# The attention's state product in a mixture-of-experts layer: one product of 128 columns written as four of 32

## What is computed

```python
def step(S, inp):
    q_t, k_t, v_t, gk_t = inp
    S = jnp.exp(gk_t)[..., None] * S + k_t[..., None] * v_t[..., None, :]
    o_t = jnp.einsum('bhdv,bhd->bhv', S, q_t) * SCALE
    return (S, o_t)
...
o = o * jax.lax.rsqrt(jnp.mean(o * o, axis=-1, keepdims=True) + EPS) * g_norm_w
o = o.reshape(Bb, Ll, Hid)
g = x @ Wg
o = o * (g * jax.nn.sigmoid(g))
o = o @ Wo
...
h = h + _L0_attn_ref(_layernorm(h, axis=-1), ...)
h = h + _L0_ffn_ref(_layernorm(h, axis=-1), ...)
```

## Time and profile before

| | |
|---|---|
| median of three runs | 635.37 us |
| lowest, highest | 631.81, 639.4 us |
| span of the profiled execution | 629.6 us |
| its own device time | not listed apart from the runs; the median stands 5.8 us above the span |
| PE matmuls busy | 585.3 us, 93% |
| PE weight loads busy | 548.2 us, 87% |
| DVE, ACT, GpSimd busy | 379.6, 337.5, 308.1 us |
| mean granted TensorE clock | 0.974 |

### The profile page before, as it was taken

One profiled execution on the slowest core, in us unless ns is written; L12 is line 12 of the kernel. 1 busy time (PEld: TensorE's weight loads), 2 busy tenths in 40 slices (PEclk: granted clock), 3 DMA queues, 4 the chain that ended last, 5 costly groups with the idle time before them and its releaser, 6 DMA issues.

```text
span 629.6 us, 14269 instructions
## 1 busy us (share of the span) xinstructions
PE 585.3 (93%) x5044; PEld 548.2 (87%) x5044; DVE 379.6 (60%) x1000; ACT 337.5 (54%) x889; POOL 308.1 (49%) x370
## 2 busy tenths in 40 slices
PE   5999999999989989739999999999999999999993
PEld 5998889789977776538899999999999999999993
DVE  4756668877765869745553736637457275473540
ACT  4687678546666756223464626537356274462530
POOL 6002222110545188534176967568575775767323
PEclk9999999999999999865999999999999999999998
DMA  7992012012313001121565171550824607333003
GB/s 206 276 320 90 12 41 89 4 60 68 118 39 104 23 22 35 52 79 56 181 197 106 47 222 18 176 108 22 236 26 144 140 1 246 38 89 54 10 7 42
DMA packets 44875, 59.89 MB, mean 95 GB/s; under 512 B 5184, under 2 KB 33424, under 8 KB 44816
## 3 DMA queue, kind: packets, MB, share of 16 engines
q1 hardware_dynamic: 37136, 49.28, 25.5%
q0 software_dynamic: 7680, 9.86, 9.2%
HBM read 41.07 MB, written 18.05 MB: 94 GB/s over the span
## 4 chain that ended last, share of the span: by engine, by line
PE 87%; DVE 5%; issue 3%; ACT 1%; another core or an unknown queue 1%; DMA 0%; DVEq 0%; POOL 0%; SPq 0%; POOLq 0%
PE ps L1928 49%; PE ps L1975 14%; PE ps L2150 3%; PE ps L2164 3%; PE ps L2109 3%; PE ps L1970 2%; PE ps L2054 2%; PE ps L2145 2%; PE ps L1949 1%; PE ps L2179 1%; PE ps L2157 1%; PE ps L2125 1%; PE ps L2072 1%; DVE sb_att L1698 1%; PE ps L2198 1%
## 5 line engine op out<-in xcount | busy, mean ns | idle before, releaser
L1928 PE MATMUL ps<-sb_xe_hi,sb_rounded 128*128 128x256 f32 (+1 forms) x1024 | 211.2, 299 | 0.2 <-DVE sb_dec L1433 0.2
L1928 PEld LDWEIGHTS ps<-sb_xe_hi,sb_rounded 128*128 128x128 f32 x1024 | 167.4, 190 | 3.0 <-issue 2.3
L1928 PE MATMUL ps<-sb_xe_lo,sb_rounded 128*128 128x320 f32 (+1 forms) x512 | 151.7, 296 | 0.0
L1928 PEld LDWEIGHTS ps<-sb_xe_lo,sb_rounded 128*128 128x128 f32 x512 | 97.2, 190 | 0.0
L1433 DVE TENSOR_TENSOR sb_dec<-ps,sb_gate 128x256 f32<-128x256 f32 (+1 forms) x121 | 55.2, 456 | 66.8 <-ACT sb_gate L1135 61.2
L1975 PE MATMUL ps<-sb_rounded,sb_h_hi 128*128 128x256 f32 x512 | 94.3, 285 | 0.0
L1135 ACT ACTIVATE sb_gate<-ps 128x256 f32<-128x256 f32 (+1 forms) x121 | 49.2, 406 | 71.8 <-PE ps L1928 70.9
L1975 PEld LDWEIGHTS ps<-sb_rounded,sb_h_hi 128*128 128x128 f32 x512 | 78.2, 189 | 0.0
L980 POOL DMA_INDIRECT out_rows<-sb_att,sb_s_token x40 | 61.8, 1545 | 28.1 <-DVE sb_att L1444 19.2
L1975 PE MATMUL ps<-sb_rounded,sb_h_lo 128*128 128x256 f32 x256 | 71.9, 281 | 0.0
L1463 DVE TENSOR_TENSOR sb_h_lo<-sb_dec,sb_h_hi 128x256 fp32r<-128x256 f32 x128 | 66.5, 520 | 1.9 <-ACT sb_h_hi L1398 1.1
(11 more groups left out here) (216 smaller groups left out, 1110.9 us busy)
## 6 DMA issues: line engine op xcount, KB each, us to landing
sb_x_in<-in_x SPq DMA_DIRECT2D x16, 512.0 KB, 4.8
sb_raw<-in_L_ffn_W SPq DMA_DIRECT2D x16, 512.0 KB
sb_x_in<-in_L_ffn_W SPq DMA_DIRECT2D x16, 512.0 KB
xe_rows<-sb_xr SPq DMA_DIRECT2D x3, 1457.5 KB, 14.2
sb_att<-xe_rows SPq DMA_DIRECT2D x32, 132.5 KB, 2.3
sb_xn<-in_L_ffn_W SPq DMA_DIRECT2D x8, 512.0 KB
sb_h<-in_L_ffn_W SPq DMA_DIRECT2D x8, 512.0 KB
out_rows<-sb_h SPq DMA_DIRECT2D x16, 128.0 KB, 2.1
```

The lines of the kernel that those rows point to most:

```text
L1928: ins = pe.matmul(out_ap, lhs, rhs, start=(first and i == 0), stop=(last and i == n - 1))
```

## The change

It touches the mix on PE alone. For a tile of 128 tokens the state's product of 128 columns becomes four products of 32 columns, each of which writes its strip of 32 partitions, as the attention's products do; each is put ahead of its half's 8 products. For the tile of 32 tokens the product stays as it is, but those of both halves now stand ahead of all the others. Only the first half's state product starts the accumulation in the bank (`start=(hf == 0)`). What is multiplied and added is the same.

```diff
                     else:
                         need("pool", "q_mask", b, 0)
                         need.once(consts, CONSTS)
+                    old = state[:, c % 2, :, :] if c else state0[:, b % 2, :, :]
+                    queries = zq[b % 2][:, :, ST[c]:ST[c] + r]
+                    if r < P:
+                        for hf in range(DT):
+                            pe.matmul(bank[:, hf * r:(hf + 1) * r], old[:, hf, :], queries[:, hf, :],
+                                      start=(hf == 0), stop=False, skip_group_check=True)
                     for hf in range(DT):
                         cols = slice(hf * r, (hf + 1) * r)
-                        pe.matmul(bank[:, cols], state[:, c % 2, hf, :] if c else state0[:, b % 2, hf, :],
-                                  zq[b % 2][:, hf, ST[c]:ST[c] + r], start=True, stop=False, skip_group_check=True)
+                        for j in range(4 if r == P else 0):
+                            at_j = slice(32 * j, 32 * j + 32)
+                            pe.matmul(bank[at_j, cols], old[:, hf, at_j], queries[:, hf, :],
+                                      start=(hf == 0), stop=False, skip_group_check=True)
                         for e in range(2):
                             for j in range(4):
                                 v48 = vp[b % 2][0:r, c, 4 * hf + j, :, :].rearrange("p a v -> p (a v)")
```

## The result

| measured | median us (lowest to highest) | kernel before beside it | ratio, 95% interval |
|---|---|---|---|
| the change | 635.11 (629.28 to 644.4) | 637.89 | 0.9924 [0.9898, 0.9951] |
| again (`after_again`) | 633.97 (630.69 to 640.08) | 637.61 | 0.9965 [0.9936, 0.9993] |
| a third time (`after_third`) | 635.03 (628.45 to 639.39) | 637.7 | 0.9954 [0.9902, 1.0006] |

A forecast was written before the change was run, and what follows sets the result against it. PE was taken to bound the kernel, busy nearly throughout 8 to 228 us. Terms 5.3 + 0.7 + 0.8 + 0.3 + 1.3 = 8.4 us, 3.4 lost, 5.0 off 635.37 gives 630.4 us; range 625.5 to 637.

The forecast's parts named there:

- Inside the full mixes, 0.33 each: In each of 16 full mixes the pair of shape changes between the halves goes: 0.33 us each, 5.3 on PE.
- Behind another mix: Two mixes directly behind another mix also lose the pair of shape changes between them: 2 x 0.33 = 0.7 us.
- Behind scores: Four mixes following a scores step start attention 0.22 us behind the state product instead of 0.42: 4 x 0.20 = 0.8 us.
- The 32-token tiles, 0.34 each: Four tiles of 32 tokens, both wide state products put ahead of all narrow records: 0.34 us saved each, 1.3 in all.
- The hand-overs: Places after 97 us where PE waits for just-in-time suppliers, mostly DVE; 3.4 us of PE's gain lost there.
- 5.0 of 8.4 pass: Of 8.4 us saved on PE over all mixes, 5.0 reach the kernel's end.
- Rival 4, code fetch, 0.12: Added instructions shift PE's code-fetch stops: one more of 2.4 us gives 632.8, one fewer 628; chance 0.12 with more stops.
- Rival 3, the sequencer: In the mixes the sequencer cannot feed the denser records: 10.6 us slower on PE, 642 at the end; chance 0.07.
- the rule weighed there: Skill's about 62 ns per MATMUL: a full mix 3.0 us against 2.0, kernel some 15 us slower; trace judged against it.
- Rival 1, everything passes: All of PE's 8.4 us saving in the mixes reaches the end, giving 627.0 us; chance 0.17.
- PE's busy time down by 8: Sign that the forecast is right: PE's busy time over the profile falls by some 8 us.
- Experts 5 us earlier: Sign that the forecast is right: the experts, after the attention and routing, begin some 5 us earlier.

The follow-up runs named there:

- batch3: The kernel before with the change made in batch 3's mixes alone; ratio to the kernel before 0.998 [0.9933, 1.0027].
- after_shift: The change with 96 TensorE instructions fewer inside batch 0's never-taken exact path; 630.74 us, ratio to the kernel before 0.9869.
- hoist_wide: The kernel before with both 128-column state products of every mix put ahead of its narrow products, not split; 633.48 us, ratio 0.9917.
- before_shift: The kernel before with 160 TensorE instructions fewer inside batch 0's never-taken exact path; 638.92 us, ratio 1.0006.
- hoist_b0: The change, but batch 0's state products stay wide, ahead of its narrow ones; 631.08 us, ratio to the kernel before 0.9871; again 631.33, 0.988.
- before_pad96: The kernel before with 96 semaphore increments, which nobody waits for, at the head of PE's program; 648.48 us, ratio 1.0145.
- split_wide: The kernel before with each wide state product cut in two over 64 queries each, 4 attention products behind each piece; 655.56 us, ratio 1.0302.

## Why the prediction was right

The forecast of 630.4 from 635.37, 0.8%, was right in class and nearly in size: 0.76, 0.35 and 0.46% came. But the sum hit in part because two errors met.

- **Inside the full mixes, 0.33 each:** right, 0.34. Behind another mix: right, 0.65 a step instead of 1.00. Behind scores: the attention starts 118.04 - 117.80 = 0.24 behind the state's first record, forecast 0.22, before 0.42.
- **The 32-token tiles, 0.34 each:** the term that was mis-sized, 0.25. The sum on PE is then about 8.1, not 8.4.
- **The hand-overs:** of those named, the ones in batch 3 came as computed (1.01 and 0.34), and `batch3` shows the same wait of 2.85 and no gain that its interval could tell. The list missed one: PE's step L2165 waits for ACT's squares, 1.71 us at 215.64, 0.62 in `after_shift`, where the kernel before had no wait. The mix had got faster, and the work on its output hadn't.
- **5.0 of 8.4 pass:** without the stop, `after_shift` is 7.0 us under the kernel before in the medians (637.7 to 630.74), 5.7 to 11.0 by its interval. So by that interval at least 5.7 of 8.1 pass, more than the 5.0 of 8.4 let through; and `hoist_wide`, 0.9917, gives 5.3 us of 6.3. PE's work counts for more than the single profile, with its just-in-time hand-overs, suggested.
- **Rival 4, code fetch, 0.12:** it happened, beside the forecast. One stop came new, as it says, but not where I looked: it read the earlier trace rows as code fetch, and that stop inside mix 2.1 is in `after_shift` and `before_shift` alike, whose code lies elsewhere, so it isn't the place of the code. The real one stands behind a branch, lasts 1.43 to 1.62 instead of 2.4 us, and in two of the change's three profiles brings a stretch at 1.2 GHz, worth 2.9 us, that no term had. In these profiles it takes 1.4 to some 4.4 us of the gain; 2 to 5 are left in the ratios. So the total came near the forecast with the stop that the sum left out set against hand-overs that cost less than the sum said: that is luck.
- **Rival 3, the sequencer:** wrong. 48 records start within 64.89 - 63.44 = 1.45 us, not the 3.0 that the rule weighed there would give, and a half's 24 in 0.66, 0.0275 each as computed. Rival 1, everything passes, is nearer to the truth than I gave it, for the kernel without the stop.
- **The signs:** "PE's busy time down by 8" was a bad one, since low clock makes records longer. "Experts 5 us earlier" needed two executions of equal luck.

## What to carry to other kernels

Products that take different shapes of the array should be grouped by shape, and reordering does most of what rewriting them does: 0.33 us for each pair of changes saved. A gain read off the timeline is a local sum; before the total is believed, look at what the added instructions push behind them, above all at branches. Here a jump taken soon after PE had entered a block of code, or one that landed 48 or fewer instructions before a block's end, cost 1.0 to 1.6 us, and in some executions 2.9 more in clock. Shifting code that never runs (here 96 instructions of an untaken path) is a test that isolates this, and a variant of another length (`hoist_b0`) can be the faster kernel for that reason alone.

## What the runs showed of the hardware that was not expected

- A block of code takes 2.3 to 2.6 us from its packet to its first instruction, on PE, in the eight profiles with the stop.
- The clock fell behind the stop in five of the eight profiles, among them the third of the change (0.68 over 110 to 118 us) and `before_shift` (0.77), but not in the change's first, in `before_pad96` or in `split_wide`; so a stop doesn't always cost clock. What decides it wasn't tested.
- The stop in pieces inside mix 2.1 or right behind it, around 200 to 220 us, is in every profile. It sums to 1.3 to 1.7 us in `batch3`, `before_shift`, `before_pad96` and `split_wide`, and to 2.4 to 3.0 in the kernel before and all others. What sets its length stays open. GpSimd's indirect writes of rows (L1069) run at that time; that they cause it was not tried.
- 96 semaphore increments at the head of PE's program delayed its first matmul by 9.4 us, 0.1 us each.
